# Experts of layers 0 and 2 on gathered tokens, with the back products of four experts side by side in the array

## The reference, cut to what matters

```python
def _L0_ffn_ref(x, gate_w, w_gate, w_up, w_down):       # CAPACITY = 2, E = 8, S = 128
    k = S // E * CAPACITY                               # 32 tokens for each expert
    affinity = softmax(einsum('bsd,ed->bse', x, gate_w)).transpose(0, 2, 1)
    gating, idx = top_k(affinity, k)                    # each expert picks its own tokens
    x_in = x[bidx, idx]
    h = silu(einsum('bekd,eid->beki', x_in, w_gate)) * einsum('bekd,eid->beki', x_in, w_up)
    x_e = einsum('beki,edi->bekd', h, w_down)
    out = zeros_like(x).at[bidx, idx].add(gating[..., None] * x_e)

def _L2_ffn_ref(x, Ws, bs, W1, b1, W2, b2):             # N = 128, E = 8
    k = int(1.0 * N / E)                                # 16 tokens for each expert
    route_prob = softmax(xf @ Ws + bs).T
    route_vals, routes = top_k(route_prob, k)
    h = gelu(einsum('ekd,edf->ekf', xf[routes], W1) + b1[:, None, :])
    out = (einsum('ekf,efd->ekd', h, W2) + b2[:, None, :]) * route_vals[..., None]
    final = zeros((N, D)).at[routes.reshape(-1)].add(out.reshape(-1, D))
```

## Time and profile before

| what | value |
|---|---|
| three runs | 3181.72, 3187.33 and 3190.36 us; median 3187.33 us |
| the profiled execution | 3184.66 us, of which the span is 3182.9 us |
| busy share of the span | TensorE 91%, its weight loads 76%, VectorE 58%, ScalarE 42%, GpSimd 13% |
| mean granted TensorE clock | 0.921 of full speed |
| expert stage of layer 0 | 775.6 to 880.3 us of the span |
| expert stage of layer 2 | 1741.3 to 1821.2 us of the span |

### The profile page before, as it was taken

One profiled execution on the slowest core, in us unless ns is written; L12 is line 12 of the kernel. 1 busy time (PEld: TensorE's weight loads), 2 busy tenths in 40 slices (PEclk: granted clock), 3 DMA queues, 4 the chain that ended last, 5 costly groups with the idle time before them and its releaser, 6 DMA issues. The chain is left out here.

```text
span 3182.9 us, 66757 instructions
## 1 busy us (share of the span) xinstructions
PE 2882.6 (91%) x27158; PEld 2426.1 (76%) x27158; DVE 1842.5 (58%) x3245; ACT 1340.0 (42%) x2197; POOL 408.3 (13%) x575
## 2 busy tenths in 40 slices
PE   7999789995979995779996789999999999999968
PEld 6999647773947775647774758999999999999857
DVE  5665478865268873568882424555555555555433
ACT  4555347770137772237772203344334434434311
POOL 3444300001000000000000022020110202000000
PEclk9999879997979996879997859999999999999869
DMA  5889697733687741577751623010101010000026
GB/s 170 329 305 344 256 239 187 185 95 112 238 191 182 187 116 30 203 180 190 179 136 48 214 70 82 1 41 1 41 1 41 1 41 1 1 1 1 18 75 218
DMA packets 193698, 394.02 MB, mean 124 GB/s; under 512 B 30480, under 2 KB 161937, under 8 KB 182638
## 3 DMA queue, kind: packets, MB, share of 16 engines
q1 hardware_dynamic: 179853, 344.12, 37.0%
q10 hardware_dynamic: 13540, 45.60, 3.7%
HBM read 290.13 MB, written 99.52 MB: 122 GB/s over the span
## 5 line engine op out<-in xcount | busy, mean ns | idle before, releaser
L878 DVE TENSOR_REDUCE L_xattn_tops<-psum 128x1 f32<-128x896 f32 x672 | 704.6, 1084 | 176.5 <-PE psum L704 174.8
L801 ACT ACTIVATE L_xattn_probs<-psum 128x512 f32<-128x512 f32 x1176 | 612.5, 601 | 343.9 <-PE psum L717 341.6
L1877 DVE TENSOR_SCALAR_CACHE_REDUCE L_units_raw<-psum 128x448 f32<-128x448 f32 x448 | 277.4, 619 | 461.2 <-PE psum L1793 458.7
L1837 ACT ACTIVATE L_units_raw<-L_units_raw,L_units_negmax 128x896 f32<-128x896 f32 x224 | 221.7, 1037 | 592.4 <-DVE L_units_negmax L1887 592.4
L1813 PE MATMUL psum<-wide_tokens,L_units_high 128*128 128x386 f32 x1568 | 456.9, 358 | 1.4 <-DVE L_units_low L1896 1.4
L704 PE MATMUL psum<-L_xattn_keys,L_xattn_q_stack 96*128 96x448 bf16 (+1 forms) x1344 | 389.1, 373 | 58.4 <-DMA L_xattn_q_stack<-query_parts 22.9
L717 PEld LDWEIGHTS psum<-L_xattn_q_stack,L_xattn_keys 99*128 99x128 bf16 (+1 forms) x4704 | 308.0, 98 | 169.7 <-issue 76.6
L717 PE MATMUL psum<-L_xattn_q_stack,L_xattn_keys 99*128 99x128 bf16 (+1 forms) x4704 | 405.8, 222 | 6.3 <-POOL L_xattn_q_stack L850 2.2
L1814 PE MATMUL psum<-wide_tokens,L_units_low 128*128 128x194 f32 x1568 | 395.5, 252 | 0.0
L733 PE MATMUL psum<-L_xattn_probs,L_xattn_values 128*17 128x128 f32 x9408 | 330.8, 276 | 2.2 <-issue 2.0
L1813 PEld LDWEIGHTS psum<-wide_tokens,L_units_high 128*128 128x128 f32 x1568 | 294.8, 188 | 11.2 <-DVE L_units_low L1896 1.6
(11 more groups left out here) (449 smaller groups left out, 3985.7 us busy)
## 6 DMA issues: line engine op xcount, KB each, us to landing
key_parts<-proj_parts SPq DMA_DIRECT2D x84, 672.0 KB, 4.4
L_xattn_keys<-key_parts SPq DMA_DIRECT2D x252, 224.0 KB, 4.4
L_xattn_keys<-key_parts SPq DMA_DIRECT2D x252, 168.0 KB, 3.6
L_ffn_w<-in_L_ffn_W SPq DMA_DIRECT2D x32, 1024.0 KB, 5.6
values_scratch<-held ACTq DMA_DIRECT2D x12, 1904.0 KB, 10.1
L_xattn_values<-values_scratch SPq DMA_DIRECT2D x45, 476.0 KB, 6.9
values_scratch<-proj_values ACTq DMA_DIRECT2D x9, 1904.0 KB, 9.1
L_ffn_w<-in_L_ffn_w SPq DMA_DIRECT2D x16, 1024.0 KB, 7.2
```

Of the source, the lines that this page charges most:

```text
L801: act.activation(group_probs(k), score_bank(k), ACT.Exp).then_inc(sem("probs"), 1)
L878: dve.tensor_reduce(tops[:, h % 2, 2 * c + w:2 * c + w + 1], top_slot(n), AX.XY, ALU.max)\
L1837: act.activation(half, half, ACT.Exp, bias=new).then_inc(sem("probs"), 1)
L1877: dve.tensor_scalar(raw[u % 2][:, s * SUB:s * SUB + width], bank(g, s % 2, 0, width), 0.0, None, ALU.add, ALU.max, accum_out=tops[:, h, s: ...
```

## The change

In layers 0 and 2 the self-attention stage and the expert stage are now made by one function, `gathered_experts`. It opens the tiles for all expert weights around both stages. `load_ahead`, called at the end of SyncE's list in the attention stage, loads only the router weights and the biases there, because the argument `ahead` is 0. All 24 (layer 0) or 16 (layer 2) loads of 1 MB are issued from the start of the expert stage, with no wait on a buffer except for `w2` of experts 4 to 7 in layer 0, which go into the `w1` tiles of experts 0 to 3. Layers 1 and 3 keep `expert_ffn`.

The expert stage first finds the tokens. From `picked` it then computes each token's place in its expert's list by a product with a triangular matrix (`rank`), sets up a one-hot tile `slots` of 128 x (8 experts x 32 places), and gathers with a matmul: `xgT` = `xn` times `slots`. Inner products, activation and back products work on 32 columns for each expert, in layer 2 too, where 16 of them are empty. Only then do the inner products start. A unit is now a whole expert with 256 elements of activation for each partition. The back products of experts 0 to 3 write to partitions 0, 32, 64 and 96 of one bank, the next four to another bank, and a product with `scatterT` spreads each group over the 128 tokens with its weights.

```diff
+            @block.sync
+            def _(sp):
+                for name, e in LOADS[ahead:]:
+                    if name == w2 and e >= G and not ALL_W2:
+                        sp.wait_ge(sem("inner_in_psum"), e - G + 1)
+                    load_weights(sp, name, e)
...
+                pe.wait_ge(sem("slots"), 1)
+                for k in range(DG):
+                    last = pe.matmul(bank(g, 5, k * E * SL, (k + 1) * E * SL), g.xn[:, k * 128:k * 128 + 128],
+                                     slots[:].rearrange("t e s -> t (e s)"), start=True, stop=True, skip_group_check=True)
...
+                def inner_products(e):
+                    pe.wait_ge(landed(f"w1_{e}"), W1_LANDED)
+                    at_least(pe, sem("act"), e - 1)
+                    for out, buf in ((inner_bank(e), w1_buf), (up_bank(e), up_buf))[:2 if w_up else 1]:
+                        for j in range(FG):
+                            for k in range(DG):
+                                col = k * FF + j * 128
+                                last = pe.matmul(out[:, j * SL:j * SL + SL], buf[:, e, col:col + 128],
+                                                 xgT[:, k, e * SL:e * SL + SL], start=(k == 0), stop=(k == DG - 1),
+                                                 skip_group_check=True)
+                    last.then_inc(sem("inner_in_psum"), 1)
+
+                def back(half):
+                    mine = range(half * G, half * G + G)
+                    for e in mine:
+                        pe.wait_ge(landed(f"w2_{e}"), 16)
+                    pe.wait_ge(sem("act"), half * G + G)
+                    for j in range(FG):
+                        for e in mine:
+                            rows = slice(e % G * SL, e % G * SL + SL)
+                            last = pe.matmul(bank(g, 4 + half, 0, D)[rows, :], act_out[:, e, j, :],
+                                             w2_of(e)[:, j * D:j * D + D], start=(j == 0), stop=(j == FG - 1),
+                                             skip_group_check=True)
+                    last.then_inc(sem("back"), 1)
+
+                def spread(half):
+                    pe.wait_ge(sem("y"), half + 1)
+                    pe.matmul(bank(g, 6, 0, D), scatterT[:, half, :], y[half][:], start=(half == 0 and not b2),
+                              stop=(half == 1)).then_inc(sem("spread"), 1)
+
+                for e in range(G + 1):
+                    inner_products(e)
+                    if e == 1:
+                        pe.wait_ge(sem("scatter"), 1)
+                        for half in range(2):
+                            last = pe.transpose(bank(g, 4, half * T, half * T + T),
+                                                scatter[:, half * G:half * G + G, :].rearrange("t e s -> t (e s)"), g.ident)
+                        last.then_inc(sem("scatterT_in_psum"), 1)
+                pe.wait_ge(sem("scatterT"), 1)
+                back(0)
+                if b2:
+                    pe.matmul(bank(g, 6, 0, D), weightsT[:], b2_rows[:], start=True, stop=False)
+                for e in range(G + 1, E):
+                    inner_products(e)
+                spread(0)
+                back(1)
+                spread(1)
...
-    "a0": wavelet_mixing, "f0": expert_ffn(0, **EXPERTS[0]),
+    "a0": gathered_experts(0, wavelet_mixing, 0, **EXPERTS[0]),
...
-    "a2": rotary_attention, "f2": expert_ffn(2, **EXPERTS[2]),
+    "a2": gathered_experts(2, rotary_attention, 0, **EXPERTS[2]),
```

203 lines of the change are left out of this document (added).

## The result

The changed kernel takes 3226.96 us (median of 4 runs, 3216.43 to 3227.69), the kernel before, run beside it, 3184.52 (4 runs, 3177.05 to 3190.36): a ratio of 1.0127, with a 95% interval from 1.0096 to 1.0158, so **1.3% slower**. The forecast was 3227. The profiled execution of the changed kernel is its fastest, 3216.43 us, with a span of 3214.7; against the profiled span of before, 3182.9, that is +31.8 us.

What follows compares the result with a forecast made beforehand. TensorE was taken to set the pace, with narrow pairs paid by weight loads at half clock. Layer 0 +34, layer 2 +5 and the rest +1 gave +40 us on the median 3187.33: 3227 us, range 3203 to 3258.

Steps and rivals of the forecast that it cites:

- The price of a narrow pair and the clock: Inner products of both stages: weight load alone sets the price, 0.213 us a pair, at a granted clock of 0.50.
- the four windows of the earlier trace: Narrow or mixed TensorE stretches before the change, at clock 0.50, cited as evidence that narrow streams don't lift it.
- The near bound of a pair: Inner products: lowest price of a load and product pair, 0.112 us, at the full clock.
- The head of layer 0: Start of layer 0's expert stage: search plus 4.7 us of new steps, inner products starting 14.5 us in.
- The back groups: Back products of both expert stages: four experts side by side, 64 instructions in 7.5 us a group.
- The credit for the clock: Both expert stages: back products may lift the clock, 5 us taken off each, bounds 0 and 10 us.
- Rival B: Both expert stages: clock up for about half the narrow work, 38 us back, 3188 us, no change; chance 5%.
- When the loads end: Expert weight loads: DMA idle after 61 us in layer 0 and 41 us in layer 2, nothing waiting behind the first expert.
- long past: Layer 0: `w2` of experts 4 to 7 waits only for inner products finished well before.
- Layer 3's head: Start of layer 3 after layer 2's experts: no change, since TensorE waits for a load first.
- Layer 1's cross-attention: Stage after layer 0's experts: starts with the clock low where it was high, +0.6 us.
- The sum: Whole kernel: +34 in layer 0, +5 in layer 2, +1 elsewhere, +40 us in all, 3227 us, 1.3% slower.

Runs made afterwards that it cites:

- the last experiment: Changed kernel with layer 0's tokens held, 512 weight columns streamed, 20 of 24 loads ahead, layer 2 streaming 128 columns: 3124.17 us, 0.9807 of the kernel before.

## Why the prediction was right, step by step

**The price of a narrow pair and the clock: right.** 6.83 us for 32 pairs is the 0.213 us read from the earlier trace rows, and the clock was 0.50 from the first inner product to the first back group, as in the four windows of the earlier trace rows on which the forecast rested. The experiments with 128, 96 and 64 columns show it to be the width of the stream, with the same loads and instructions. An expert came every 13.65 us in layer 0, forecast 13.6.

**The near bound of a pair: right too.** At 2.4 GHz, with 64 to 128 columns, 32 pairs take 3.58 us, 0.112 each, beside 0.213 at 1.2 GHz. The Trainium skill's page "TensorE: Matmul & The Clock Gate" (section "LDWEIGHTS (loading the stationary operand)") would have 0.107 us, an estimate by its rule, at either level; these runs agree with it at the upper level alone.

**The head of layer 0: right.** Inner products began 14.5 us into the stage, forecast 14.5; the new chain from `picked` to them was 4.9 us, forecast 4.7. In layer 2 it was 13.1, forecast 13.

**The back groups: right in kind.** The forecast had 7.5 us at the lower clock; the half group of 3.64 us at 0.51 in the last experiment gives 7.3 for a whole one. In the changed kernel they took 5.74 and 4.49 us, since the clock rose within them. At the full clock, in the kernel with 128 columns, a group took 3.66 us for 64 instructions: 0.057 each, against 0.21 for the same width one after the other in the earlier trace rows. The Trainium skill's page "TensorEngine Tiling (Array Packing)" (section "Theoretical Speedup") gives up to four times for 32 columns held; these are 3.7 times.

**The credit for the clock: the term of the sum that was mis-sized.** Taken as 5 us in each stage. In layer 0 the two groups behind the first back group gave 3.25 + 1.64, the back groups 7.3 − 5.74 and 7.3 − 4.49, together 9.3: so +30.0 instead of +34. In layer 2 the 96 products took 16.40 instead of 20.5 and the back groups 5.68 and 5.07: 8.0 in place of 5, and +1.0 instead of +5; 0.7 of these 4 are the transposes and the product with `b2`, 1.1 us where I had 1.8. Both credits lie inside the bounds given (0 and 10). In the profile of layer 2 alone the credit was smaller and the stage grew by 5.3. Rival B, with half of the narrow work at the full clock, had the right effect and far too much of it: the narrow products' part of the credit, 9.0 us at 0.1 us a pair, is an estimated 90 of the 768 pairs.

**When the loads end: wrong, at no cost.** I had the DMA engines idle after 61 and 41 us. They were busy to about 75 and 46 us. The last `w2` of layer 0 waits for the inner products of expert 3, which by the forecast's own steps end 69 us into the stage, so they are not "long past" when its turn comes. No product waited for it.

**Layer 3's head: the step that failed.** I wrote "nothing in layer 3's, where TensorE waits for a load first". The wait itself grew, from 16 to 21 us, and the stretch to layer 3's experts by 4 us. TensorE's clock had nothing to do with it (behind the 128 columns the wait is 23.8 us); the transfers and their issue did. Layer 1's cross-attention, where I had +0.6 for a clock that starts low, took 353.8 and 352.9 us before and 354.5 and 354.4 after. But it took 354.6 too behind the 128 columns, whose stage ends with products at the full clock, so that this is the clock's isn't shown.

**The sum.** By the profile −0.6 ahead of layer 0's stage, +30.0, −1.4 up to layer 2's attention stage, +0.4 in it, +1.0, and +2.4 behind: +31.8. Forecast was +40; the second profile of the changed kernel gives +37.7, and the medians differ by 42. The two stages, forecast at +39, came to +31. That the forecast met the median to the microsecond is luck: 8 us too much in the stages stand against the 2.4 behind them, which were not foreseen, and some 10 between the profile and the medians that no trace places.

## What to carry to other kernels

Here products that held a full 128x128 block of float32 and streamed 32 to 128 columns were paid by their block loads, and the clock decided between 0.213 and 0.112 us for each; look in the trace for a stretch as narrow as the new one and read its clock before counting columns as a saving. If the narrow form is wanted, pad the stream until the clock stays up (72 us here), or better hold the narrow operand and stream the wide one with four column groups side by side, which here brought the inner products of a layer from 107 to 21 us and left the loads from memory as the bound. Once TensorE is that fast, the order of those loads, and which buffers they must wait for, is the next thing to plan.

## What the hardware showed that was not expected

What the clock did depended on what it was before: in the inner products with 96 and 128 columns it rose from 0.50 to 1.00; with 64 it stayed at 1.00 behind the back products (six groups at 3.74 to 3.79 us) and at 0.50 ahead of them (ten groups at 6.93 to 7.06 us); with 32 it fell from 1.00. With 32 and with 64 columns TensorE and its loads were busy in 68 of 68 us at 0.50.

With the same instructions in layer 2's stage the time that the clock stays up behind a back group differs between profiles: 96 narrow products took 16.40 and 16.07 us in the changed kernel and 18.92 in the one with the change in layer 2 alone.

The same 7.89 MB of loads, in 5264 packets and in the same order, went at 232 GB/s in the kernel before and 205 in the changed one, and one issue among them took 1.68 us instead of 0.42. This stays unexplained.
